# Two cross-attention and MoE layers on one core: the second attention layer's value product in float32

## The reference

```python
q_in = x @ Wq + _lora(x, q_down, q_up, q_alpha)          # 16 heads of 64
org_ctx, ipa_ctx = context[:, :end, :], context[:, end:, :]   # 371 and 4 tokens
k_in = org_ctx @ Wk + _lora(org_ctx, k_down, k_up, k_alpha)
v_in = org_ctx @ Wv + _lora(org_ctx, v_down, v_up, v_alpha)
out = _attention(q_in, k_in, v_in)                       # softmax(q k^T / 8) v
out = out + _attention(q_in, ipa_ctx @ Wk_ipa, ipa_ctx @ Wv_ipa)
return out @ Wo + bo + _lora(out, o_down, o_up, o_alpha)
```

## Time and profile before

| | us |
|---|---|
| median of 3 runs | 1244.21 (1240.41 to 1251.22) |
| profiled execution, whole time | 1243.78 |
| its span | 1242.1 |
| PE busy in it | 1062.8 (86%) |
| DVE busy | 848.7 (68%) |
| ACT busy | 531.8 (43%) |
| POOL busy | 278.2 (22%) |

### The profile page before, as it was taken

How to read it: one execution, slowest core, us unless ns; L and a number is a source line. 1 busy time by engine, 2 the same in 40 slices (tenths; PEclk the granted TensorE clock), 3 DMA queues, 4 the chain that set the end, 5 groups by cost and what they waited for, 6 DMA issues and landing times.

```text
span 1242.1 us, 21550 instructions
## 1 busy us (share of the span) xinstructions
PE 1062.8 (86%) x7860; PEld 729.1 (59%) x7860; DVE 848.7 (68%) x1624; ACT 531.8 (43%) x996; POOL 278.2 (22%) x272
## 2 busy tenths in 40 slices
PE   0699999982979999853688999999985899999997
PEld 0488888882635555642356766776664555555553
DVE  5455555547298888697567777777765667776774
ACT  3355555551333343441465656665652422222220
POOL 1422222202155563001000100000010023333341
PEclk9999999985599999996799999999998699999999
DMA  5000000001113122321000000000001131122101
GB/s 196 1 1 2 0 0 0 0 2 68 65 49 97 51 92 64 124 68 34 6 1 2 1 2 1 1 0 1 1 1 59 49 127 66 65 67 102 43 1 30
DMA packets 9931, 47.79 MB, mean 38 GB/s; under 512 B 1513, under 2 KB 3313, under 8 KB 6930
## 3 DMA queue, kind: packets, MB, share of 16 engines
q1 hardware_dynamic: 9874, 47.03, 11.3%
HBM read 45.92 MB, written 1.11 MB: 38 GB/s over the span
## 4 chain that ended last, share of the span: by engine, by line
PE 48%; DVE 20%; issue 16%; ACT 8%; POOL 6%; DMA 2%; DVEq 0%; POOLq 0%; ACTq 0%
PE pb L1192 7%; PE tp L645 5%; PE sp L631 5%; POOL qz L1285 5%; PE pb L587 5%; PE sp L1177 4%; PE tp L1177 4%; PE pb L662 4%; PE pb L608 2%; DVE ST L888 2%; PE pb L581 2%; ACT ST L767 2%; DVE nm L894 1%; DVE ST L891 1%; ACT ST L764 1%
## 5 line engine op out<-in xcount | busy, mean ns | idle before, releaser
L1285 POOL TENSOR_TENSOR qz<-qz,Z 128x448 f32<-128x448 f32 x128 | 169.3, 1332 | 284.6 <-ACT qz L1224 193.5
L1192 PE MATMUL pb<-V,KT 128*128 128x448 f16 x816 | 161.4, 355 | 7.3 <-DVE V L1264 7.3
L774 ACT ACTIVATE ST<-tp 125x672 f32<-125x672 f32 (+1 forms) x128 | 93.5, 730 | 149.7 <-PE tp L645 149.7
L1177 PE MATMUL sp<-xT,KT 128*128 128x448 f16 x624 | 135.8, 359 | 0.0
L1177 PE MATMUL tp<-xT,KT 128*128 128x448 f16 x624 | 133.3, 354 | 2.7 <-DVE qz L1255 2.7
L631 PE MATMUL sp<-KT,qz 128*112 128x375 f16 (+1 forms) x768 | 116.8, 331 | 15.4 <-ACT ST L767 13.2
L1192 PEld LDWEIGHTS pb<-V,KT 128*128 128x128 f16 x816 | 80.1, 98 | 83.6 <-DVE V L1264 8.4
L1264 DVE TENSOR_TENSOR V<-qz,V 128x448 f16<-128x448 f32 x136 | 117.5, 864 | 4.7
L645 PE MATMUL tp<-identf,ST 112*125 112x112 f32 x768 | 112.5, 283 | 6.7 <-ACT ST L764 4.2
L645 PEld LDWEIGHTS tp<-identf,ST 112*125 112x125 f32 x768 | 96.1, 189 | 32.9 <-issue 17.1
L1262 DVE CAST V<-qz 128x448 f16<-128x448 f32 x136 | 94.9, 698 | 23.1 <-POOL qz L1285 19.5
(11 more groups left out here) (215 smaller groups left out, 1720.2 us busy)
## 6 DMA issues: line engine op xcount, KB each, us to landing
ST<-in_moe SPq DMA_DIRECT2D x9, 1536.0 KB, 7.9
ST<-in_moe SPq DMA_DIRECT2D x8, 1024.0 KB, 6.8
Z<-wd_scratch SPq DMA_DIRECT2D x16, 448.0 KB, 4.6
ST<-in_ctxT SPq DMA_DIRECT2D x4, 750.0 KB, 5.0
ST<-in_gens SPq DMA_DIRECT2D x2, 768.0 KB, 4.9
ST<-in_lora SPq DMA_DIRECT2D x2, 624.0 KB, 9.7
ST<-in_w1q SPq DMA_DIRECT2D x1, 1024.0 KB
ST<-in_w1k SPq DMA_DIRECT2D x1, 1024.0 KB
```

Of the source, the lines that this page charges most:

```text
L774: act.activation(PT[:, st % 2, :, 0, :] if l else PT0[:, st % 2, :, :], TP2[0:CHUNK, :, 0:NCH * S], ACT.Copy)\
L1177: mm = pe.matmul(banks[m % len(banks)][:, 0:HT], MW[:, es % 2, qa, c:c + 128], xT[:, qb, k, half * HT:(half + 1) * HT], start=(i == 0), st ...
L1192: mm = pe.matmul(SUM[half][c][:, 0:HT], MW[:, es % 2, qa, c0:c0 + 128], HTt[:, half, qb, k, :], start=False, stop=(es == n - 1 and i == last))
L1285: pool.tensor_tensor(tile, tile, wdB[:, es % 2, half * HT:(half + 1) * HT], ALU.mult)\
```

## The change

The second layer now does what the first one did, with its own width:

- `PT` is gone. ACT copies the turned probabilities as float32 (`PT0`); DVE's `lo` is gone. What waited for `lo_done` waits for `hi_done`.
- A v unit is one DVE instruction from PSUM to float32 values `V1` in place of one of ACT and one of DVE.
- The value product of a head is three float32 matmuls with 64 columns.
- Eight heads fill a bank; there are two groups a batch, divided after p=5 and p=1. DVE writes 1/sum and then multiplies straight from PSUM. POOL's `divide` and the adding of halves are gone.
- The image tokens' values stay whole (no low part), in one transfer, and PE's wait ahead of the layer is for ACT's copy of them.

```diff
-        self.grouped = 512 // (2 * dim)
+        self.grouped = 8 if index else 16
@@ attention_tensor
-                pe.wait_ge(s["lo_done1"] if l else s["hi_done0"], i + 1)
+                pe.wait_ge(s[f"hi_done{l}"], i + 1)
                 for j, h in enumerate(L.pairs[p]):
                     for c in range(NCH):
-                        if l == 0:
-                            mm = pe.matmul(psum_out(L, gs, h), PT0[:, st % 2, j, c * S:(c + 1) * S],
-                                           V0[0:CHUNK, bs % 2, c, h, :], start=(c == 0), stop=(c == NCH - 1))
-                            continue
-                        for qa in range(2):
-                            mm = pe.matmul(psum_out(L, gs, h), PT[:, st % 2, j, qa, c * S:(c + 1) * S],
-                                           V[0:CHUNK, bs % 2, :, c, h * L.dim:(h + 1) * L.dim],
-                                           start=(c == 0 and qa == 0), stop=(c == NCH - 1 and qa == 1))
+                        values = V0[0:CHUNK, bs % 2, c, h, :] if l == 0 else \
+                            V1[0:CHUNK, bs % 2, c, h * L.dim:(h + 1) * L.dim]
+                        mm = pe.matmul(psum_out(L, gs, h), PT0[:, st % 2, j, c * S:(c + 1) * S], values,
+                                       start=(c == 0), stop=(c == NCH - 1))
@@ attention_scalar
-                elif u[0] == "v":
-                    m = min(CHUNK, L.keys - u[1] * CHUNK)
-                    act.activation(V[0:m, bs % 2, 0, u[1], u[2] * 512:u[2] * 512 + L.vw], bank[0:m, 0:L.vw],
-                                   ACT.Copy, scale=1.0 / WS).then_inc(g_hi, 1)
@@ attention_vector
-                    x = dve.scalar_tensor_tensor(V[0:m, bs % 2, 1, u[1], c], bank[0:m, 0:L.vw], 1.0 / WS,
-                                                 V[0:m, bs % 2, 0, u[1], c], *step)
+                    x = dve.tensor_scalar(V1[0:m, bs % 2, u[1], u[2] * 512:u[2] * 512 + L.vw], bank[0:m, 0:L.vw],
+                                          1.0 / WS, None, ALU.mult)
-                dve.scalar_tensor_tensor(PT[:, st % 2, :, 1, :], TP2[0:CHUNK, :, 0:NCH * S], 1.0,
-                                         PT[:, st % 2, :, 0, :], *step).then_inc(s[f"lo_done{l}"], 1)
-                halves = OBK[gs % 2][0:S, :].rearrange("p (h q d) -> p h d q", h=L.grouped, q=2)
-                dve.tensor_reduce(ob, halves, AX.X, ALU.add).then_inc(s[f"halves{l}"], 1)
+                dve.wait_ge(s["r_done1"], group + 1)
+                dve.tensor_tensor(ob, OBK[gs % 2][0:S, :].rearrange("p (h d) -> p h d", h=L.grouped),
+                                  bc(rinv[:, heads].unsqueeze(2), [S, L.grouped, L.dim]), ALU.mult)\
+                   .then_inc(s["o_rd1"], 1)
@@ ahead of the layer
-            pe.wait_ge(s["ipa_lo"], 3)
+            pe.wait_ge(s["ipa_lo"], 1)
+            pe.wait_ge(s["ipa_hi"], 3)
```

More of the change, by code:

```diff
@@ L81, in __init__ @@
         self.k_units = [("k", t) for t in range(self.tiles)]
-        self.v_units = [("v" if index else "w", c, w) for c in range(NCH) for w in range(self.width // self.vw)]
+        self.v_units = [("v", c, w) for c in range(NCH) for w in range(self.width // self.vw)]
         self.i_units = [("i",)] if index else []
@@ L114, in acts @@
 def acts(u):
-    return u[0] not in ("i", "o", "w")
+    return u[0] not in ("i", "o", "v")
 def build(nc, a, out):
@@ L246, in build @@
         for L in range(2):
-            for n in """s_mm clip_done qz_done mx_done exp_done t_mm hi_done lo_done pv_mm g_mm g_hi g_free
+            for n in """s_mm clip_done qz_done mx_done exp_done t_mm hi_done pv_mm g_mm g_hi g_free
                     o_rd r_done x_up ipa_patch ipa_sc ipa_z ipa_m ipa_e ipa_s ipa_r ipa_pn vi_in""".split():
@@ L263, in build @@
         V0 = VF[:, 0:4 * NCH * H * 17].bitcast(F32).rearrange("p (a c h d) -> p a c h d", a=2, c=NCH, h=H)
+        V1 = VF[:, :].bitcast(F32).rearrange("p (a c n) -> p a c n", a=2, c=NCH)
         PT0 = flat[0:CHUNK, 2528:2528 + 4 * NCH * S].rearrange("p (a j n) -> p a j n", a=2, j=2)
@@ L475, in psum_out @@
                 return OBK[group % 2][0:S, h * 17:(h + 1) * 17]
-            c = (h % L.grouped) * 2 * L.dim
-            return OBK[group % 2][0:S, c:c + 2 * L.dim].rearrange("p (q d) -> p q d", q=2)
+            c = (h % L.grouped) * L.dim
+            return OBK[group % 2][0:S, c:c + L.dim]
         def counts(L):
@@ L581, in unit @@
                         mm = pe.matmul(bank[:, 0:L.keys], w, c, start=(i == 0), stop=(i == 4))
-                elif u[0] in ("v", "w"):
+                elif u[0] == "v":
                     m = min(CHUNK, L.keys - u[1] * CHUNK)
@@ L641, in turn @@
                 if st >= 1:
-                    pe.wait_ge(s["lo_done1"] if l else s["hi_done0"], i)
+                    pe.wait_ge(s[f"hi_done{l}"], i)
                 for j in range(2):
@@ L773, in hi @@
                     act.wait_ge(s[f"pv_mm{l}"], i - 1)
-                act.activation(PT[:, st % 2, :, 0, :] if l else PT0[:, st % 2, :, :], TP2[0:CHUNK, :, 0:NCH * S], ACT.Copy)\
+                act.activation(PT0[:, st % 2, :, :], TP2[0:CHUNK, :, 0:NCH * S], ACT.Copy)\
                    .then_inc(s[f"hi_done{l}"], 1)
@@ L830, in unit @@
                                                  kT[bs % 2][0][:, u[1], 0:L.keys], *step)
+                elif u[0] == "v" and l == 1:
+                    m = min(CHUNK, L.keys - u[1] * CHUNK)
+                    x = dve.tensor_scalar(V1[0:m, bs % 2, u[1], u[2] * 512:u[2] * 512 + L.vw], bank[0:m, 0:L.vw],
+                                          1.0 / WS, None, ALU.mult)
                 elif u[0] == "v":
-                    m = min(CHUNK, L.keys - u[1] * CHUNK)
-                    c = slice(u[2] * 512, u[2] * 512 + L.vw)
-                    x = dve.scalar_tensor_tensor(V[0:m, bs % 2, 1, u[1], c], bank[0:m, 0:L.vw], 1.0 / WS,
-                                                 V[0:m, bs % 2, 0, u[1], c], *step)
-                elif u[0] == "w":
                     x = dve.tensor_scalar(V0[0:CHUNK, bs % 2, u[1], :, 0:16],
@@ L976, in attention_gpsimd @@
                 return
[L977 to L984, removed]
             def patches(bv, bs):
@@ L994, in patches @@
                         .then_inc(s["ipa_patch1"], 1)
[L995 to L998, removed]
             patches(0, 0)
@@ L1011, in attention_sync @@
                     sp.wait_ge(s["pv_mm1"], (b - 1) * NP)
-                for q in range(2):
-                    sp.dma_start(V[CHUNK - IPA:CHUNK, b % 2, q, NCH - 1, :],
-                                 vi_dram[b * IPA:(b + 1) * IPA, q, :]).then_inc(s[f"vi_in{b % 2}"], 16)
+                sp.dma_start(V1[CHUNK - IPA:CHUNK, b % 2, NCH - 1, :], vi_dram[b * IPA:(b + 1) * IPA, :])\
+                    .then_inc(s[f"vi_in{b % 2}"], 16)
         cI = [[cT[:, q, k, :].rearrange("p (b n) -> p b n", b=B)[:, :, ORG:KV] for k in range(2)] for q in range(2)]
-        vi_sb = flat[0:B * IPA, 4800:5312].bitcast(F16)
-        vi_sb2 = flat[0:B * IPA, 5312:5824].bitcast(F16)
+        vi_sb = flat[0:B * IPA, 4800:5824]
         ci_sb = KT[:, 8192:8192 + 4 * B * IPA].rearrange("p (q k n) -> p q k n", q=2, k=2)
@@ L1053, in ipa_vector @@
                                      ALU.mult, ALU.subtract).then_inc(s["ipa_lo"], 1)
[L1054 to L1058, removed]
         def router_tensor(pe, l, turned):
@@ L1649, in _ @@
             chunks_sync(sp, NC0, NC1)
[L1650 to L1653, removed]
+            sp.wait_ge(s["ipa_hi"], 3)
+            sp.dma_start(vi_dram, vi_sb).then_inc(s["ipa_stored"], 16)
+            sp.wait_ge(s["ipa_stored"], 16)
             attention_sync(sp, layers[1])
```

22 lines of the change are left out of this document (6 added, 16 removed).

## The result

| | before | after |
|---|---|---|
| median, us | 1247.22 (4 runs, 1240.41 to 1251.22) | 1273.55 (4 runs, 1271.46 to 1280.10) |
| span of the profiled execution | 1242.1 | 1273.8 |
| mean granted TensorE clock | 0.939 | 0.922 |

The ratio is 1.0226, with a 95% interval of 1.016 to 1.0291. The forecast was 1254 in a range of 1245 to 1267. The kernel became slower by 26 us where 10 were forecast. What follows shows that a middle batch at full clock costs what was forecast to 0.14 us, and that most of the rest is a lower clock of TensorE, of which the forecast had no term. All medians, ratios and intervals are without one execution of before_q_earlier, which took 1890.5 us at a mean clock of 0.551.

The account below looks back on a forecast made before the run. PE was taken to bound the layer, 36.9 of a 40.67 us period plus stalls at fixed places. Six middle batches +11.5, first +0.8, last +0.45, edges -2.8 made +10.0, so 1254 us, range 1245 to 1267.

Parts of the forecast that it names:

- The product's price: Second layer's value product on PE: 1.11 us a pair for 0.67 before, about 0.45 more with the slower first load.
- That 64 columns hide: Value product: 64 float32 columns stay behind the weight loads at 93 ns a record; the rival, 109 ns, had 0.25.
- What the stalls swallow: Eight steps of a middle batch: PE's existing stalls absorb part of the 0.45 a product, leaving 1.91 us a batch.
- The stall before the third key unit: PE's 1.55 us wait in p=1 for DVE's key cut: absorbs that product's growth whole, about 1.1 left.
- The one before the scores of p=4: PE's 0.81 us wait for an exponential behind the image tokens' chain on ACT: absorbs the growth, 0.36 left.
- The chain behind the large stall: The wait before the third key unit begins at the query units, ahead of the product, through ACT's and DVE's cuts.
- DVE and ACT: Work off the bounding engine gets lighter: DVE about 21.5 of 40 us, ACT 20 or so.
- Edges: Layer's start and end: -0.7 at the start, -1.2 ahead of the first scores, -0.9 at the end, together -2.8 us.
- the first part's "at full clock (1.00)": What bounds the kernel: in a middle batch of the second layer, PE busy 38.53 of 40 us at 2.4 GHz.

Follow-up runs that it names:

- before_q_earlier: Kernel of before with the image tokens' score unit behind p=4's product and the first query unit ahead of p=0's: 1241.39 us (0.9954), again 1241.02 (0.9945).
- apart_lo_kept: after_i_apart with DVE's `lo` instruction kept, its result unused and the next turn waiting for it: 1260.56 us, ratio 1.0110 to the kernel of before.
- apart_q_earlier: after_i_apart with the first query unit one slot earlier, ahead of the value product of p=0: 1260.79 us, ratio 1.0108 to the kernel of before.
- after_again: The changed kernel measured once more, unaltered: 1271.87 us, ratio 1.0205 to the kernel of before.
- before_i_twice: Kernel of before, float16 product, with the 32 8-column matmuls of the image tokens' scores issued twice: 1278.85 us, ratio 1.0272.
- after_cols128: Changed kernel in its own order, 128 columns for 64 in each float32 matmul of the second layer's value product: 1260.60 us, ratio 1.0134 to before.
- after_i_apart: Changed kernel with the image tokens' score unit moved from p=4 to p=6, a value unit put into p=4 instead: 1259.18 us, ratio 1.0121 to before.

## Why the prediction was wrong, step by step

- **The product's price.** Forecast 1.11 to 1.12 us a pair, measured 1.14. That 64 columns hide was right, nearly: a record takes 95 ns for the 93 with 17.
- **What the stalls swallow.** Forecast 1.91 us of growth a batch; the one at full clock has 42.72 for 40.67, 2.05 more. The stall before the third key unit was to shrink to 1.1: the key unit at 728.25 in the changed kernel's PE timeline should be over at 729.04, the next starts at 730.13, 1.09. The one before the scores of p=4 was to shrink to 0.36: the transposes start at 837.96 and take 0.37, the scores start at 838.63, so 0.30. That DVE's smaller busy time matters no further is borne out by apart_lo_kept; for ACT it is not tested. The chain behind the large stall was read rightly only in part: it begins at the query units, but at the second of them, which stands behind the product (apart_q_earlier).
- **DVE and ACT.** Forecast about 21.5 and 20 of 40 us; at full clock 20.6 to 21.3 and 19.8 to 20.3.
- **Edges.** From the first query unit to the mark of the first batch it took 31.66 us before (608.11 to 639.77) and 30.40 after (609.74 to 640.14), -1.26 for the forecast -1.2. Ahead of it the listed idle went from 1.44 to 0.97, -0.5 for the forecast -0.7. From the mark at 882.97 to the last projection at 951.59 it took 68.6 before, and 69.3 after (911.98 to 981.26), +0.7. By the forecast it should be 1.9 for the last middle batch, 0.45 for the last one and -0.9 at the end, +1.5. The missing 0.8 is nearly all a fall in the trace of before: the eight transposes at 948.49 took 1.73 us there at the low clock, and 0.96 after.
- **The step that failed** is the first part's "at full clock (1.00)", read from a middle batch of before and carried over unsaid to the changed kernel: the change of the clock stood at nothing in the sum, and no rival had one. What the runs showed in its place is the clock at half for 6.8 to 10.2 us in five of the eight batches of the first profile, each time beginning 2.4 to 4.4 us after the start of the image tokens' unit. The sum of the trace is this. Five middle periods grew by 25.6 us (203.65 to 229.25): 10.0 from the product, 15.6 from the falls. The first batch grew by 3.0, 0.8 of it forecast. The start gives 1.3 back, the end adds 0.7. That is 28.0 in the layer. The stages ahead of the first query unit and behind the last projection add 1.6 and 2.0. They are unchanged but for the image tokens' values, and scatter by more than that: the first query unit began anywhere from 603.0 to 611.2 us in the traces of this study. So about 18 of the 31.7 us between the two profiles are falls of the clock, 3.6 are other stages, and 10 remain for the change itself. That this is the forecast's number is in part luck: the five periods cost 0.4 more than forecast (10.0 for 9.6), and the end cost 0.8 less through a fall in the trace of before.

The Trainium skill warns of a lower clock in "TensorE: Matmul & The Clock Gate" (Why this matters for your kernels), but by gaps in which TensorE is idle. By that rule nothing was to be feared here, since the change fills stalls. The trace doesn't agree: from 740 to 748 PE is listed busy without a gap, and the clock falls.

Could the trace of before have told it? Partly. Its middle windows stand at 1.00, with the same unit of 8 columns and a product of 128 columns at 56 ns behind it. But its first batch has a fall behind this very unit. One window and the timeline of PE of before:

```profile
640.00:680.00 40.00, 36.67 (x347) 26.58 (x345) 29.03 (x50) 24.10 (x60) 3.47 (x11) 0.96 0.01 2
```

```profile
650.58 1.77 PE L595 MATMUL pb<-KI,qz 128*112 128x8 f16 x32
...
654.08 1.18 PE L631 MATMUL sp<-KT,qz 64*112 64x371 f16 x6 [1.02 <-ACT ST L767]
```

The scores take 1.11 us to the next group there (0.61 at full clock), behind the unit, the product and 1.02 us in which PE stands still. So the place was near a fall before the change. The change took the columns of the product from 128 to 64 a record and gave it 1.7 times the time. That should have raised the question; what the place would bear, the trace did not say.

What stays open is why, with equal work, some batches fall and others don't (47.4 and 42.7 us in one execution), and why the same ones do in two executions.

## What to carry to other kernels

Count what a change does to the columns per microsecond that TensorE streams, not only to its busy time. An instruction form bound by its weight loads keeps PE busy and lightens its stream, and next to another light stretch that cost the clock here. Such stretches are worth keeping apart: reordering the same instructions gave back 12.7 of the 27.5 us between after_again and the kernel of before. Look for falls in every stretch of the trace of before, not in one middle window. A stall swallows the growth of a piece only where the wait's chain begins ahead of that piece; the two large ones here were read off like that to 0.1 us.

## What the runs showed of the hardware

- The granted clock fell from 1.00 to 0.50 with PE listed busy throughout (after, 744.7 us), behind 32 matmuls of 8 columns and twelve float32 records of 64. It also fell behind 64 matmuls of 8 columns with a float16 product (before_i_twice, 745 to 750 at 0.66). It held in the profiled execution with 128 columns in the same records (after_cols128; 1260.60 us against 1271.87).
- In the batches of the orders with the unit in p=6, falls began 1.0 to 1.8 us after the start of the 32 matmuls of 8 columns, ahead of a float32 product (apart_lo_kept three, apart_q_earlier two, after_i_apart one).
- A plain float32 matmul with 112 weights is two records of 93 ns with 17 columns, 95 with 64, and 109 with 128. That fits the greater of its load and two clocks a column.
